# Six of attention's forty squares on VectorE, in two instructions each, with the normaliser's reciprocals in four pieces and the count differences between them

## What is computed

```
xn  = layernorm(x)
gnn = segment_mean(xn[src], dst) @ W_l.T + xn @ W_r.T + b_r
mix = Taylor attention, 8 heads of 32: q, k, v = xn @ Wqkv.T + bqkv
      q, k normalised to length 1 and scaled, v = v / 625
      y = 0.5*(q.k)^2 v + sqrt(32)*(q.k) v + 32*v, summed over the nodes
      y / y_norm                      # the same sum with v = 1
      mix = y @ Wproj.T + bproj
x   = x + gnn + mix
x   = x + ffn(layernorm(x))           # 8 experts, each node takes one
```

## Time and profile before

| | us |
|---|---|
| median of three runs | 250.19 |
| the profiled execution | 250.31 |
| its span, first to last instruction | 248.6 |
| TensorE busy | 234.3 (94%) |
| VectorE busy | 146.3 (59%) |
| ScalarE busy | 145.8 (59%) |
| attention, first score matmul to first transpose of the counts | 92.17 to 125.39 |

### The profile page before, as it was taken

The page is one execution under the profiler, slowest core; times in us unless marked ns, Lnnn a source line. Parts: engine busy times, 40 slices in busy tenths (PEclk is TensorE's granted clock), DMA queues, the critical chain, the costliest instruction groups (busy, mean ns, idle before and its releaser), DMA issues.

```text
span 248.6 us, 4705 instructions
## 1 busy us (share of the span) xinstructions
PE 234.3 (94%) x1422; PEld 148.8 (60%) x1423; DVE 146.3 (59%) x415; ACT 145.8 (59%) x224; POOL 31.8 (13%) x64
## 2 busy tenths in 40 slices
PE   7799999999997999999999999998899999999990
PEld 2448676665454553333388886573455578888870
DVE  2999999999999969940144649524600243323320
ACT  3998999999999968899940116433143332333000
POOL 7470000000000029000000000000630000000331
PEclk9999999999999999999999999999999999999999
DMA  6660000000000000399900000130123000000111
GB/s 233 193 220 3 1 3 5 3 3 7 3 3 3 3 3 3 96 423 423 402 12 3 1 0 0 33 134 0 38 73 107 0 1 3 0 1 3 39 34 32
DMA packets 6030, 15.82 MB, mean 64 GB/s; under 512 B 2724, under 2 KB 3783, under 8 KB 4723
## 3 DMA queue, kind: packets, MB, share of 16 engines
q1 hardware_dynamic: 4432, 12.64, 13.8%
q0 software_dynamic: 1280, 1.31, 2.0%
q10 hardware_dynamic: 288, 1.44, 1.4%
HBM read 14.08 MB, written 1.30 MB: 62 GB/s over the span
## 4 chain that ended last, share of the span: by engine, by line
PE 75%; DVE 18%; DMA 2%; ACT 1%; issue 1%; POOL 0%; DVEq 0%; ACTq 0%
PE ps L1283 17%; DVE mem L735 11%; PE ps L1221 7%; PE ps L1103 7%; PE ps L980 7%; PE ps L1267 6%; PE ps L1017 5%; PE ps L1124 5%; PE ps L1183 4%; DVE mem L738 4%; PE ps L1251 3%; PE ps L1172 2%; PE ps L1174 2%; DMA edges_sb<-in_edges 2%; PE ps L1019 1%
## 5 line engine op out<-in xcount | busy, mean ns | idle before, releaser
L529 ACT ACTIVATE mem<-ids_m,half_src 128x628 bf16<-128x628 f16 x97 | 70.6, 813 | 0.0
L1017 PE MATMUL ps<-mem 128*128 128x501 bf16 x177 | 50.2, 374 | 1.7 <-issue 1.5
L735 DVE TENSOR_SCALAR mem<-node_ids,dst_f 128x628 bf16<-128x628 f16 x157 | 51.6, 383 | 0.0
L1283 PE MATMUL ps<-mem 128*125 x192 | 41.6, 379 | 0.0
L1283 PEld LDWEIGHTS ps<-mem 128*125 128x125 f32 x192 | 36.0, 188 | 5.4
L1019 PE MATMUL ps<-mem 128*128 128x126 bf16 x177 | 38.7, 219 | 0.0
L629 ACT ACTIVATE qk_sb<-ps,sc_col 125x626 f32<-125x626 f32 (+1 forms) x40 | 28.6, 778 | 3.7 <-PE ps L1103 3.7
L1017 PEld LDWEIGHTS ps<-mem 128*128 x177 | 17.3, 98 | 21.6 <-issue 3.9
L738 DVE TENSOR_SCALAR mem<-ids_m,src_f 128x628 bf16<-128x628 f16 x60 | 23.1, 386 | 0.0
L678 ACT COPY mem<-mem 128x1000 f32 x8 | 8.2, 1030 | 19.8 <-PE ps L1283 19.8
L1103 PE MATMUL ps<-mem 32*125 32x313 f32 (+1 forms) x160 | 19.1, 472 | 0.2 <-DVE mem L808 0.2
(11 more groups left out here) (204 smaller groups left out, 279.4 us busy)
## 6 DMA issues: line engine op xcount, KB each, us to landing
mem<-in_wd SPq DMA_DIRECT2D x8, 1024.0 KB, 13.1
w_sb<-in_w SPq DMA_DIRECT2D x1, 1024.0 KB, 8.6
vz<-in_bd SPq DMA_DIRECT2D x1, 1000.0 KB
wqkv_sb<-in_w_qkv ACTq DMA_DIRECT2D x1, 768.0 KB, 6.1
x_all<-in_x ACTq DMA_DIRECT2D x1, 640.0 KB, 4.7
row<-rows_sorted SPq DMA_DIRECT2D x1, 579.7 KB
wlr_sb<-in_w_lr SPq DMA_DIRECT2D x1, 512.0 KB, 5.4
bqk_all<-in_b_qk SPq DMA_DIRECT2D x1, 256.0 KB, 4.6
```

What stands on the lines that cost most here:

```text
L529: ins = nc.scalar.activation(oh[:, g % OHB, 0, j, :], ids_m1[:, :], ACT.Sign, bias=half_src[:, g * GC + j:g * GC + j + 1])
L735: ins = nc.vector.tensor_scalar(oh[:, g % OHB, 1, j, :], node_ids[:, :], dst_f[:, col:col + 1], None, ALU.is_equal)
L1017: mm(psf[:, bass.ds(tile * BANK, TW + 1)], node_of, oh[:, buf, 0, j, 0:TW + 1], start=False, stop=False, skip_group_check=True)
L1283: ins = mm(ps[0:TP, 4 + n % EB, 0:C], hT_step[:, n % EB, k, :], wd_sb[:, bass.ds(e, 1), k, :], start=(k == 0), stop=(k == KH - 1))
```

## The change

Six of the 40 units go to VectorE: the second unit of steps 2, 7, 11, 13, 16 and 18 (units 5, 15, 23, 27, 33, 37). VectorE has no instruction with bias and square in one, so a unit takes two: `s + c` from PSUM to a buffer `s_raised` in SBUF, and the product of that with itself into `gsq`, with a wait between the two. It has a semaphore `g_ready_v` of its own; `wait_squared(u)` has TensorE wait on the one or the other by how many units of that engine come up to u. `values` now waits for its two units one by one. ScalarE leaves out those six.

The reciprocal of the normaliser is taken in four pieces of 313 or 312 columns, and the work of VectorE in attention is put in a new order: piece 0, unit 5, piece 1, `vs`, leave block 0, difference 0, unit 15, differences 1 to 3, leave block 1, unit 23, difference 4, unit 27, `cnt`, piece 2, leave block 2, unit 33, piece 3, unit 37, leave block 3.

```diff
--- before.py
+++ after.py
@@ -157,6 +157,7 @@
         bd_all = vz_flat[:, 0:E * C]
         v_sum = row[:, 0, 0:C]
         NGB = 4
+        s_raised = big[0:TP, 0:2 * HW].rearrange("p (i n) -> p i n", i=2)
         gsq = qk_sb[0:TP, 0:NGB * 2 * HW].rearrange("p (b i n) -> p b i n", b=NGB, i=2)
         yT_sb = sb("yT_sb", [P, T * 2 * (P + 1)])
         yT = yT_sb[:, 0:2 * N].rearrange("p (k n) -> p k n", k=2)
@@ -247,6 +248,7 @@
         scales_ready = sem("scales_ready")
         A_done = sem("A_done")
         A_copied_a = sem("A_copied_a")
+        norm_ready = sem("norm_ready")
         A_copied_v = sem("A_copied_v")
         A_ready = sem("A_ready")
         b7_full = sem("b7_full")
@@ -273,6 +275,7 @@
         xb_ready = sem("xb_ready")
         s_ps = sem("s_ps")
         g_ready = sem("g_ready")
+        g_ready_v = sem("g_ready_v")
         g_used = sem("g_used")
         y_ready = sem("y_ready")
         y_left = sem("y_left")
@@ -391,6 +394,15 @@
 
         units = [(hg, hf, m, pr) for hg in range(2) for hf in range(2) for m in range(T) for pr in range(2)]
         SLOTS = 3
+        DVE_TILES = ((2,), (2,), (1, 3), (1, 3))
+
+        def on_dve(u):
+            hg, hf, m, pr = units[u]
+            return m in DVE_TILES[2 * hg + hf] and pr == 1
+
+        def squared(u):
+            return sum(on_dve(n) == on_dve(u) for n in range(u + 1))
+
         LN_PARTS = ((0, 2), (2, T))
 
         block = ctx.enter_context(nc.Block())
@@ -620,6 +632,8 @@
                     nc.scalar.copy(sums, banks).then_inc(A_copied_a, 1)
 
             for u, (hg, hf, m, pr) in enumerate(units):
+                if on_dve(u):
+                    continue
                 lo, hi = HALF[hf]
                 w = hi - lo
                 act.wait_ge(s_ps, u + 1)
@@ -807,30 +821,65 @@
                 if n not in ACT_SUMS:
                     nc.vector.tensor_copy(sums, banks).then_inc(A_copied_v, 1)
             dve.wait_ge(b7_free, JOBS)
-            step(nc.vector.reciprocal(rn[:, 0, :], rn[:, 0, :]))
-            dve.wait_ge(A_copied_a, 2)
-            dve.wait_ge(A_copied_v, 5)
-            for t in range(T):
+
+            def normaliser(k):
+                lo, hi = HALF[k % 2]
+                nc.vector.reciprocal(rn[:, k // 2, lo:hi], rn[:, k // 2, lo:hi]).then_inc(norm_ready, 1)
+
+            def squares(u2):
+                u = 2 * u2 + 1
+                lo, hi = HALF[units[u][1]]
+                dve.wait_ge(s_ps, u + 1)
+                if u >= NGB:
+                    dve.wait_ge(g_used, (u - NGB) // 2 + 1)
+                b = 2 * (u % SLOTS)
+                s = ps[0:TP, b:b + 2, 0:hi - lo]
+                raised = s_raised[:, :, 0:hi - lo]
+                step(nc.vector.tensor_scalar(raised, s, SC2, None, ALU.add))
+                nc.vector.tensor_tensor(gsq[:, u % NGB, :, 0:hi - lo], raised, raised, ALU.mult).then_inc(g_ready_v, 1)
+
+            def counts_of(t):
                 nc.vector.tensor_tensor(A[:, t, :], cum[:, t, 1:N + 1], cum[:, t, 0:N], ALU.subtract
                                         ).then_inc(A_ready, 1)
-            step(nc.vector.tensor_tensor(cnt[:, :], cum[:, :, N], cum[:, :, 0], ALU.subtract))
-            step(nc.vector.tensor_scalar(cnt[:, :], cnt[:, :], 2.0, None, ALU.max))
-            nc.vector.reciprocal(cnt[:, :], cnt[:, :]).then_inc(A_ready, 1)
-
-            dve.wait_ge(v_sum_ps, 1)
-            nc.vector.tensor_scalar(vs[:, :], ps[:, 7, C:C + 2], SC2 * SC2, None, ALU.mult).then_inc(v_sum_read, 1)
-            dve.wait_ge(in_bv, 16)
-            dve.wait_ge(v_sum_read, 1)
-            for k in range(4):
+
+            def left(k):
                 hg, (lo, hi) = k // 2, HALF[k % 2]
+                dve.wait_ge(norm_ready, k + 1)
                 dve.wait_ge(g_used, T * (k + 1))
                 nc.vector.scalar_tensor_tensor(yT[:, hg, lo:hi], ps[:, 6 + k % 2, 0:hi - lo], vs[:, hg:hg + 1],
                                                rn[:, hg, lo:hi], ALU.add, ALU.mult).then_inc(y_left, 1)
                 dve.wait_ge(y_left, k + 1)
                 nc.vector.tensor_scalar(yT[:, hg, lo:hi], yT[:, hg, lo:hi], bv_sb[:, hg:hg + 1], None, ALU.add
                                         ).then_inc(y_ready, 1)
-                if k == 0:
-                    step(nc.vector.reciprocal(rn[:, 1, :], rn[:, 1, :]))
+
+            normaliser(0)
+            squares(2)
+            normaliser(1)
+            dve.wait_ge(v_sum_ps, 1)
+            nc.vector.tensor_scalar(vs[:, :], ps[:, 7, C:C + 2], SC2 * SC2, None, ALU.mult).then_inc(v_sum_read, 1)
+            dve.wait_ge(in_bv, 16)
+            dve.wait_ge(v_sum_read, 1)
+            left(0)
+            dve.wait_ge(A_copied_a, 2)
+            dve.wait_ge(A_copied_v, 5)
+            counts_of(0)
+            squares(7)
+            counts_of(1)
+            counts_of(2)
+            counts_of(3)
+            left(1)
+            squares(11)
+            counts_of(4)
+            squares(13)
+            step(nc.vector.tensor_tensor(cnt[:, :], cum[:, :, N], cum[:, :, 0], ALU.subtract))
+            step(nc.vector.tensor_scalar(cnt[:, :], cnt[:, :], 2.0, None, ALU.max))
+            nc.vector.reciprocal(cnt[:, :], cnt[:, :]).then_inc(A_ready, 1)
+            normaliser(2)
+            left(2)
+            squares(16)
+            normaliser(3)
+            squares(18)
+            left(3)
 
             for n, (counts, blocks) in enumerate(at_parts()):
                 if n not in ACT_AT:
@@ -1089,6 +1138,12 @@
                 for _ in range(n):
                     mm(ps[:, b, :], zeros[:, 0:P], zeros[:, :], start=True, stop=True)
 
+            def wait_squared(u):
+                if on_dve(u):
+                    pe.wait_ge(g_ready_v, squared(u))
+                else:
+                    pe.wait_ge(g_ready, squared(u))
+
             def scores(u2):
                 hg, hf, m, _ = units[2 * u2]
                 lo, hi = HALF[hf]
@@ -1098,7 +1153,7 @@
                         pe.wait_ge(A_copied_a, (1, 2, 2)[u])
                         pe.wait_ge(A_copied_v, (1, 2, 4)[u])
                     if h % 2 == 0 and u >= SLOTS:
-                        pe.wait_ge(g_ready, u + 1 - SLOTS)
+                        wait_squared(u - SLOTS)
                     rows = slice(D * h, D * (h + 1))
                     ins = mm(ps[0:TP, 2 * ((2 * u2 + h // 2) % SLOTS) + h % 2, 0:hi - lo],
                              kT[rows, hg, TP * m:TP * (m + 1)], qT[rows, hg, lo:hi], start=True, stop=True,
@@ -1111,7 +1166,8 @@
                 hg, hf, m, _ = units[2 * u2]
                 lo, hi = HALF[hf]
                 k = 2 * hg + hf
-                pe.wait_ge(g_ready, 2 * u2 + 2)
+                wait_squared(2 * u2)
+                wait_squared(2 * u2 + 1)
                 if u2 == 0:
                     pe.wait_ge(A_copied_v, 5)
                 if k == 1 and m == 0:
@@ -1145,7 +1201,8 @@
                     ins.then_inc(v_sum_ps, 1)
                 values(u2)
 
-            pe.wait_ge(g_ready, len(units))
+            wait_squared(len(units) - 1)
+            wait_squared(len(units) - 2)
             pe.wait_ge(A_ready, T)
             pe.wait_ge(y_left, 3)
             for s in range(T):
```

## The result

The changed kernel takes 252.32 us (252.09 to 252.38, four runs), the kernel before beside it 250.23; the ratio is 1.0081, with a 95% interval of 1.0069 to 1.0093. Forecast were 252.7, a range of 251.0 to 254.0, and slower with 0.84. The profiled execution of the changed kernel took 252.38, its span is 250.6 (before 250.31 and 248.6).

A forecast was written before the change was run, and what follows sets the result against it. Attention was taken as bound by latency from scores over two squares to values. Delays of 0.56, 0.56, 0.55, 0.98 and 0.82, less 0.26 and 0.7, gave +2.5 on 250.31: 252.8, for the median 252.7 us, range 251.0 to 254.0.

The forecast's parts named there:

- The bound: Attention: neither engine but a latency, scores, first square, second square, values, then the next scores; 3.06 us for two steps.
- the forecast's point of decision: Moved units: the change pays only if VectorE's square ends within 1.14 us; its two instructions were put at 1.70.
- the second ring: Attention: scores, first square, second half of next scores, values, next scores, 3.06 us; prediction named only its wait.
- The size of a unit: Each moved square: values start 2.95 us after scores instead of 2.39, so +0.56, bounds +0.41 to +0.76.
- the start of the second unit: Moved units: VectorE can begin the second unit 1.17 us after its scores start, between 1.10 and 1.20.
- what the prediction gave as a sign of being wrong: VectorE beginning a second unit less than 0.9 us after its scores started.
- Unit 5: Step 2: the sum of v holds values until 98.89 anyway, the square would allow 98.90, so +0.
- The lock: VectorE's product in step 2 beside GpSimd additions: taken as 0, with 0.54 us kept for the range.
- The queue: VectorE behind reciprocal pieces: unit 33 starts 0.42 us late and unit 37 0.26 late; unit 23 in time.
- The rule for adding up: Steps of attention: a delay of an even step delays odd ones fully; an odd step's reaches even ones less 0.26 us.
- the return at the end: Last step of attention: values 19 follows values 18 after 0.67 us instead of 1.35, giving back 0.7.
- What was hidden: Reciprocals, differences, leaving block 3 and the later load of the experts' weights were to cost nothing; everything behind attention only moves.

The follow-up runs named there:

- the runs with less, more and no work on VectorE: The changed kernel with the six units' addition alone, 250.50 us; with their product done twice, 258.09; with all squares back on ScalarE, 250.50.
- The last two experiments: Against the kernel before, first unit's square split by heads between ScalarE and VectorE from step 8: 249.08 us; the same with VectorE's other work reordered: 248.56.
- the run with the squares ahead: The changed kernel with VectorE's six squares put before its reciprocal pieces and the leaving of blocks: 251.70 us.
- the two kernels that had them: The changed kernel with the product of the six units done twice, 258.09 us; and with VectorE taking the first unit of the six steps, 257.14 us.
- the kernel with the 1.2: The changed kernel with the product of the six units done twice in a row on VectorE: 258.09 us.
- the run without step 2: The changed kernel with VectorE taking the first unit, not the second, in five steps, step 2 left out, and one wait for undivided steps: 254.28 us.

## Why the prediction was right

*The bound.* Right that it is a latency and that VectorE's two instructions lie in it; shown by the runs with less, more and no work on VectorE. Incomplete: there are two rings of the same length. So the forecast's point of decision was wrong. It said that VectorE's square had to end within 1.14 us for the change to pay; with 0.81 it paid nothing, since the second ring stays at 3.06.

*The size of a unit.* Forecast 0.56 over ScalarE's 2.39, measured in the kernel after 0.53 and 0.32 for units 15 and 27 (2.92 and 2.71), which had no queue before them. Three terms were off: the start of the second unit (1.17 forecast; 1.12 where its scores are held, 0.90 where not), the addition (0.86 forecast, 0.81), and the way from VectorE's end to TensorE's start (0.08 taken over from ScalarE, 0.15). The product (0.81) and the gap (0.03) were right. The first of these was a misreading that happened to land close. The two rows of four in the earlier trace rows are not the two units but the first and the second record of all four heads: TensorE raises `s_ps` with the sixth and the eighth record, and in `scores(8)` these end 0.01 apart, not 0.26. The second unit is later than the first only where its half is held, by 0.27 (104.29 against 104.02), and that, with the 0.84, is the 1.12. The 0.90 lies at the edge of what the prediction gave as a sign of being wrong. The 0.15 isn't VectorE's either: from the end of ScalarE's second square of step 6 to values 6 the traces have 0.10 us in the kernel before, and 0.15, as with VectorE, in the run with all squares on ScalarE and two waits.

*Unit 5.* Forecast +0; values 2 started 99.19, which is 98.89 plus 0.27 of opening and 0.03. The lock appeared, at a smaller price: its product took 1.06 instead of 0.81; the difference in the earlier trace rows had taken 1.34. The last two experiments show it most clearly: the same five differences took 5.84 us beside GpSimd's five additions, which themselves took 5.76 there, and about 3.8 behind them (1.46 + 1.52 + 0.81), where the additions took 3.48. The Trainium skill, "SBUF — State Buffer", section "Who interferes with whom", says that a VectorE instruction with two SBUF inputs contends with a GpSimd instruction that reads SBUF, by an exclusive lock on a shared pair of ports. The traces agree in kind.

*The queue.* The scores of step 16 were held (their row above takes 1.07), so unit 33 could have started at 119.33 + 1.12 = 120.45; it started at 120.53, only 0.08 late (0.42 forecast, 0.3 in the expectation above). Unit 37, at 122.99 + 0.90 = 123.89, started at 124.11, 0.22 late (0.26). Unit 23, forecast in time, was some 0.2 late behind block 1. Together the queue cost only 0.23, by the run with the squares ahead.

*The sum.* 2.5 forecast in attention, 1.82 measured. The rule for adding up held: against the run with all squares on ScalarE values 7 came 0.49 later, values 8 only 0.19, values 9 again 0.49. The lateness against the kernel before, at values 13, 16 and 18 and at the end, was forecast as 1.67, 2.40, 3.2 and 2.5; it was 1.40, 1.73, 2.19 and 1.82. So most of the excess lay in the two even units (0.98 and 0.82 forecast, 0.59 and 0.46 measured). What went the other way was the return at the end (0.7 forecast; values 19 came 0.98 after values 18, where before it was 1.35, so 0.37) and a cost that the sum didn't have: "the new separate waits cost nothing I can see". They cost 0.35 where all steps are undisturbed, 0.04 for each held values. The row that I rested it on (`values(5)`, which already had a second wait) was of a values that TensorE itself delayed, so the wait had cover; the held ones had none. That the total came within 0.4 us of the measured time is thus in part luck: the units and the queue were put too high, the return at the end too high as well, and the waits at nothing.

*What was hidden* was hidden: reciprocals, differences, the load of the weights, block 3. Everything behind attention took 123.15 us, before 123.17.

## What to carry to other kernels

An engine that is 93% busy and one that seems 100% busy can both be waiting on a latency: add up the starts around one period before moving work, and do it for every resource that comes back round (the buffer of the result *and* the bank of the input). Moving one square to a second engine didn't pay here even where it got shorter, since a second ring of the same length was left as it was. What paid was to shorten both rings at once: splitting the first square by heads from step 8 on took 0.65% where moving whole squares lost 0.8%. The split needs two instructions on VectorE and is in time all the same, with the PSUM bank given back after the first; no run here kept the bank until after the second, so what that alone is worth isn't shown.

## What I had not expected of the hardware

- One more satisfied wait ahead of a matmul that is itself held until a square is ready cost about 0.04 us each time (1.03 instead of 0.99 after the scores), 0.35 in attention, and its removal gave 0.33 of that back.
- Waits of TensorE of 0.7 and 1.2 us at 98 to 100 us were followed by a granted clock of 0.50 (1.2 GHz) for some 3 us from 101 on, in the two kernels that had them. A later wait in the kernel with the 1.2 (1.25 us, to 110.13) left the clock at 1.00; why is open. That the early waits are the cause is argued, from the order in time and from the run without step 2, which had neither such a wait nor a lower clock.
- The second half of a scores step, alone on two of the four row groups, takes as much of TensorE as both halves together: 109.12 to 109.85 is 0.73 where it ran alone, 102.62 to 103.35 is 0.73 for a whole step. A held half is as dear as the whole.
